# Channel attention: both convolutions back to back, attention product and final product behind them, Gram product last

## What is computed

```python
mu, var = mean and variance of x over (C, H, W)      # per image
xn = (x - mu) * rsqrt(var + EPS) * ln_g + ln_b
Q, K, V = _proj(xn, ...)     # 12x12 product per head, then a 3x3 depthwise convolution, each with bias
logits = einsum('bhnc,bhnd->bhcd', K, Q) / alpha     # 8 heads of 12 channels
attn = softmax(logits, axis=-1)
out = einsum('bhnc,bhcd->bhnd', V, attn)
return einsum('bcij,oc->boij', out, w_f) + b_f + xn
```

## Time and profile before

| | |
|---|---|
| median of 3 runs | 544.88 us (543.45 to 545.36) |
| the profiled execution | 541.99 us |
| its span | 540.5 us |
| PE busy in the span | 527.2 us (98%) |
| DVE busy | 366.9 us (68%) |
| ACT busy | 318.4 us (59%) |
| POOL busy | 165.4 us (31%) |

### The profile page before, as it was taken

One profiled execution on the slowest core, in us unless ns is written; L12 is line 12 of the kernel. 1 busy time (PEld: TensorE's weight loads), 2 busy tenths in 40 slices (PEclk: granted clock), 3 DMA queues, 4 the chain that ended last, 5 costly groups with the idle time before them and its releaser, 6 DMA issues. The chain is left out here.

```text
span 540.5 us, 22584 instructions
## 1 busy us (share of the span) xinstructions
PE 527.2 (98%) x8570; PEld 335.2 (62%) x8570; DVE 366.9 (68%) x903; ACT 318.4 (59%) x781; POOL 165.4 (31%) x200
## 2 busy tenths in 40 slices
PE   8999999999999999989999999999999999999996
PEld 7777777777777777765334444458555555565553
DVE  2799999999999999964753232345556565656544
ACT  2488877777777778865993443423444444444432
POOL 8543344444434443430000000013443332333210
PEclk9999999999999999999999999999999999999998
DMA  4211111111110101000000000003454434444421
GB/s 83 55 39 42 30 30 30 29 29 29 29 29 24 26 23 43 1 4 0 0 1 0 0 0 0 0 6 83 116 154 126 113 101 116 123 111 108 114 51 32
DMA packets 36097, 26.09 MB, mean 48 GB/s; under 512 B 17241, under 2 KB 34777, under 8 KB 36057
## 3 DMA queue, kind: packets, MB, share of 16 engines
q1 hardware_dynamic: 32472, 19.81, 13.9%
q0 software_dynamic: 3584, 5.72, 4.6%
HBM read 18.36 MB, written 7.13 MB: 47 GB/s over the span
## 5 line engine op out<-in xcount | busy, mean ns | idle before, releaser
L359 POOL TENSOR_TENSOR scores<-scores,peak 128x768 f32<-128x768 f32 x64 | 94.2, 1472 | 128.5 <-DVE peak L502 128.5
L995 POOL DMA_DIRECT2D x_stack<-padded_x x96 | 52.2, 546 | 96.6 <-PE ps_v L1268 67.4
L419 ACT COPY probs_t<-ps_probs 128x768 f32<-128x768 f32 x64 | 51.1, 798 | 40.6 <-PE ps_probs L634 40.5
L494 DVE TENSOR_TENSOR scores<-ps_scores,bias 128x768 f32<-128x768 f32 x64 | 61.3, 957 | 6.1 <-PE ps_scores L624 4.3
L502 DVE TENSOR_REDUCE peak<-scores 128x12 f32<-128x768 f32 x64 | 61.0, 953 | 2.4
L647 PE MATMUL ps_out<-v_blocks,probs_t 128*64 128x54 f32 x1536 | 57.2, 224 | 1.6 <-ACT out_t L424 1.5
L647 PEld LDWEIGHTS ps_out<-v_blocks,probs_t 128*64 128x64 f32 x1536 | 50.2, 138 | 12.9 <-issue 12.9
L846 ACT ACTIVATE hidden<-ps_hidden,fc_b_folded 128x512 f32<-128x512 f32 x48 | 32.4, 688 | 42.9 <-PE ps_hidden L798 42.7
L413 ACT ACTIVATE scores<-scores 128x768 f32<-128x768 f32 x64 | 54.2, 847 | 1.5 <-POOL scores L359 1.5
L634 PE MATMUL ps_probs<-ident,scores 128*128 128x128 f32 x384 | 54.3, 277 | 0.0
L881 DVE SCALAR_TENSOR_TENSOR mixed<-ps_y,fc_b,stream 96x384 f32 (+3 forms) x32 | 13.9, 476 | 54.1 <-PE ps_y L805 54.1
(11 more groups left out here) (137 smaller groups left out, 915.4 us busy)
## 6 DMA issues: line engine op xcount, KB each, us to landing
x_stack<-padded_x SPq DMA_DIRECT2D x96, 54.0 KB
x_stack<-padded_x POOLq DMA_DIRECT2D x96, 54.0 KB, 2.7
padded_x<-x_pad SPq DMA_DIRECT2D x32, 121.5 KB, 2.5
out<-y_sb SPq DMA_DIRECT2D x32, 96.0 KB, 2.0
x_now<-in_x SPq DMA_DIRECT2D x32, 72.0 KB, 1.8
stream<-in_x SPq DMA_DIRECT2D x32, 72.0 KB, 1.9
x_now<-in_x SPq DMA_DIRECT2D x32, 24.0 KB, 1.8
stream<-in_x SPq DMA_DIRECT2D x32, 24.0 KB, 1.8
```

The source lines that it names most:

```text
L359: nc.gpsimd.tensor_tensor(sc, sc, peak[:, par, p, :].unsqueeze(2).to_broadcast((128, HEADS, WN)), ALU.subtract).then_inc(s["shifted"], 1)
L419: nc.scalar.copy(probs_t[:, :], ps_turned).then_inc(s["turned_copied"], 1)
L494: nc.vector.tensor_tensor(scores[:, par, p, :].rearrange("p (g c) -> p g c", g=NG), ps_scores[:, :, 0:GROUP * WN], bias[:, p, :].rearrange ...
L995: engine.dma_start(x_stack[64 * half + i * HC:64 * half + (i + 1) * HC, slot, :, :], rows).then_inc(landed[slot], 16)
```

## The change

The PE step for t becomes: both convolutions of image t + 1, `attend(t - 1)`, `finalise(t - 2)`, `turn_tokens(t + 1)`, the waits for image t + 2, and `gram(t)`. The first tokens are turned ahead of the loop; the final product is one image later than before. The other engines follow: ACT does the exponential of image t - 1 first and the copy of `ps_av` last, DVE copies tokens last and ends image t - 2, SP stores image t - 2. `v_sb` has four buffers and not two. No arithmetic changes.

```diff
-    v_sb = sb("v_sb", [128, 2, ROUNDS, N])
+    v_sb = sb("v_sb", [128, SLOTS, ROUNDS, N])
...
             if not past(t + SLOTS):
                 gather(sp, t + SLOTS, lap + 1, slot, 0, stacked_sp)
-            if not is_image(t, 0):
-                store(t - 1, 1 - slot % 2)
+            if not is_image(t, 0) and not is_image(t, 1):
+                store(t - 2, slot % 2)
             if not past(t + AHEAD):
                 write(t + AHEAD, (slot + AHEAD) % SLOTS)
         lap_loop(sp, step)
+        store(B - 2, 0)
         store(B - 1, 1)
...
-        def copy_v(t, par):
+        def copy_v(t, slot):
             act.wait_ge(s["v_ready"], t + 1)
-            need(act, s["av_ready"], t - 1)
-            nc.scalar.copy(v_sb[:, par, :, :], ps_v).then_inc(s["v_copied"], 1)
+            need(act, s["av_ready"], t - SLOTS + 1)
+            nc.scalar.copy(v_sb[:, slot, :, :], ps_v).then_inc(s["v_copied"], 1)
...
         def step(t, lap, slot):                                   # ACT
             if not is_image(t, 0):
-                copy_av(t - 1)
-            if not past(t + 1):
-                copy_qk(t + 1)
-            exponent(t)
+                exponent(t - 1)
             if not past(t + AHEAD + 1):
                 take_moment(t + AHEAD + 1, (slot + AHEAD + 1) % 2)
             if not past(t + 1):
-                copy_v(t + 1, 1 - slot % 2)
+                copy_qk(t + 1)
             if not past(t + AHEAD):
                 pad_x(t + AHEAD, lap + (slot + AHEAD) // SLOTS, (slot + AHEAD) % SLOTS)
+            if not past(t + 1):
+                copy_v(t + 1, (slot + 1) % SLOTS)
+            if not is_image(t, 0):
+                copy_av(t - 1)
         lap_loop(act, step)
+        exponent(B - 1)
         copy_av(B - 1)
...
         def step(t, lap, slot):                                   # DVE
-            copy_tokens(t)
+            if not is_image(t, 0):
+                shift_logits(t - 1)
             if not past(t + AHEAD):
                 take_gain(t + AHEAD, (slot + AHEAD) % 2)
-            shift_logits(t)
+            if not is_image(t, 0):
+                normalise(t - 1)
             if not past(t + AHEAD):
                 take_offset(t + AHEAD, (slot + AHEAD) % 2)
-            normalise(t)
-            if not is_image(t, 0):
-                finish(t - 1, lap * 2 + (slot // 2 if slot % 2 else slot // 2 - 1), 1 - slot % 2)
-
+            if not is_image(t, 0) and not is_image(t, 1):
+                finish(t - 2, lap * 2 + slot // 2 - 1, slot % 2)
+            if not past(t + 1):
+                copy_tokens(t + 1)
+
+        copy_tokens(0)
         lap_loop(dve, step)
+        shift_logits(B - 1)
+        normalise(B - 1)
+        finish(B - 2, B // 2 - 1, 0)
         finish(B - 1, B // 2 - 1, 1)
...
+        turn_tokens(0)
+        await_taps(1, 0, 1)
+        pe.wait_ge(s["v_copied"], 1)
+
         def step(t, lap, slot):                                   # PE
-            turn_tokens(t)
-            if not past(t + 1):
-                await_taps(t + 1, lap + (slot + 1) // SLOTS, (slot + 1) % SLOTS)
-            if not is_image(t, 0):
-                attend(t - 1, 1 - slot % 2)
             if not past(t + 1):
                 convolve(t + 1, (slot + 1) % SLOTS, 0, ps_qk, s["qk_ready"])
-                pe.wait_ge(s["v_copied"], t + 1)
-            gram(t)
-            if not past(t + 1):
                 convolve(t + 1, (slot + 1) % SLOTS, 1, ps_v, s["v_ready"])
             if not is_image(t, 0):
-                finalise(t - 1)
+                attend(t - 1, (slot + 3) % SLOTS)
+            if not is_image(t, 0) and not is_image(t, 1):
+                finalise(t - 2)
+            if not past(t + 1):
+                turn_tokens(t + 1)
+            if not past(t + 2):
+                await_taps(t + 2, lap + (slot + 2) // SLOTS, (slot + 2) % SLOTS)
+                pe.wait_ge(s["v_copied"], t + 2)
+            gram(t)
 
         lap_loop(pe, step)
-        attend(B - 1, 1)
+        attend(B - 1, (B - 1) % SLOTS)
+        finalise(B - 2)
         finalise(B - 1)
```

More of the change, by code:

```diff
@@ L1296, in gram, with attend @@
             mm.then_inc(s["gram_ready"], 1)
-        def attend(t, par):
+        def attend(t, slot):
             pe.wait_ge(s["attn_ready"], (t + 1) * ROUNDS)
@@ L1302, in attend @@
             for r in range(ROUNDS):
-                mm = nc.tensor.matmul(ps_av[64 * r:64 * r + 64, :], attn[:, r, :], v_sb[:, par, r, :], start=True, stop=True)
+                mm = nc.tensor.matmul(ps_av[64 * r:64 * r + 64, :], attn[:, r, :], v_sb[:, slot, r, :], start=True, stop=True)
             mm.then_inc(s["av_ready"], 1)
```

## The result

The changed kernel takes 547.78 us (median of 6 runs, 546.83 to 552.49) against 543.89 us (6 runs, 542.41 to 545.36): a ratio of 1.0077 [1.0048, 1.0106]. It is slower by 3.9 us. The forecast was 544.0 us with a range up to 547.2, and "slower" had 0.23.

What follows compares the result with a forecast made beforehand. PE was taken as the bound, busy all 40.00 of 40 us at full clock. Span 522.5 + 15.5 = 538.0, plus 1.2 loop and 0.4 clock, 539.6 against 540.5; hence median 544.0, range 542.0 to 547.2.

Steps and rivals of the forecast that it cites:

- "slower": Whole kernel: the rivals that end slower, softmax ring as bound (0.15) and loop and tail at upper bounds (0.08).
- The steady step: PE's six groups per step in the new order: 4.74 us against 4.91, 0.17 less.
- The loop's own overhead: Branch between gram and qk at a lap's end: 0.25 us per lap, 0.2 for entering, 1.2 in all.
- The rival that the loop hides: Lap ends: branch costs nothing and the tail keeps 2.4 GHz, span 538.0, median 542.4; chance 0.27.
- "Does PE start to wait?": Steady step: PE stays covered by tenths, margin 0.4 us for attn ahead of av, 0.7 for v's copy.
- The ring rival: Softmax chain from av to next av, 4.42 us against 4.74, becomes the bound; 0.1 beyond gives 547.0; chance 0.15.
- "Gram, behind whose wait for this copy only gram stands": PE's wait for v's copy ahead of gram: gram due at 4.37 us, copy done about 3.7, margin 0.7.
- The end: From qk 31 on: two softmax chains in series, 15.5 us against 12.2, plus 0.4 for the clock.
- the clock's term: Tail: av 31 and y 30 at the lower clock cost 0.2 to 0.3 us each; 0.4 taken, bounds 0 and 1.0.
- The start, SP, POOL and the v buffers: Stage start: first step loses 0.4 us, qk 1 nothing; SP's store, POOL's gather and v's four buffers cost nothing.

Runs made afterwards that it cites:

- tokens2: The changed kernel with two token buffers, so the token copy need not wait for gram; 546.20 us, ratio 1.0027.
- the second execution: The changed kernel itself, unaltered, profiled and timed once more; 547.85 us, ratio 1.0041 to the kernel before.
- tail: The changed kernel with another order in the last step alone, gram 31 ahead of av 30; 544.86 us, ratio 1.0002.
- before_v4: The kernel before with four buffers for v and nothing else of the change; 544.94 us, ratio 0.9995.
- unroll: The changed kernel with the five laps of the loop written out; 557.02 us, ratio 1.0206.
- tokens2_tail_unroll: The changed kernel with two token buffers, the other order in the last step and laps written out; 551.46 us, ratio 1.0125.
- between_unroll: The changed kernel, laps written out, gram between the two convolutions, v-copy wait ahead of the tokens; 562.54 us, ratio 1.0348.
- before_unroll: The kernel before with its five laps written out; 545.73 us, ratio 1.0009.
- mid_unroll: The changed kernel, laps written out, gram between attention product and final product, v-copy wait ahead of the tokens; 546.04 us, ratio 1.0018.
- behind_unroll: The changed kernel, laps written out, gram directly behind both convolutions, v-copy wait ahead of the tokens; 545.50 us, ratio 1.0009.
- split_unroll: The changed kernel, laps written out, with the v-copy wait moved from ahead of gram to between the convolutions; 544.72 us, ratio 1.0011.
- its sibling: The changed kernel, laps written out, two token buffers, other last-step order, v-copy wait between the convolutions; 540.48 us, ratio 0.9912.

## Why the prediction was wrong, by its steps

**The steady step: right.** 4.74 was forecast and 4.744 measured, and each of its terms held to 0.02, the new borders among them: av to y 0.59 (0.58 forecast), tok to gram 0.53 (0.54). What lowers the step is that qk is followed by a group of its own shape. The Trainium skill, "TensorEngine Tiling (Array Packing)", Key Properties, says that this needs no drain while a change of mode does; the trace agrees, with 1.32 against 1.46. Over 28 steps this is 4.5 us, and it was there; it was spent elsewhere.

**The loop's own overhead: right in kind, a little high.** 0.25 a lap and 0.2 for entering were forecast, 1.2 in all. Measured are 0.26 at the first lap end, 0.19 at each of the other three and 0.08 at the entry, 0.9 in all. The rows of line 898 at a lap's end (ns, start) next to the timeline:

```profile
L898 PEldq ALU_OP  x1: 32/32/32, 484.9 to 484.9; - x1
L898 PEldq COMPARE_BRANCH  x1: 215/215/215, 485.0 to 485.0; - x1
L898 PEldq MOVE  x1: 29/29/29, 485.3 to 485.3; - x1
```

```profile
484.84 0.44 PE L1304 MATMUL ps_gram<-tokens 128*32 128x12 f32 x32
...
485.40 1.53 PE L1278 MATMUL ps_qk<-x_stack,conv_w 40*32 40x256 f32 x48
```

The sequence begins at 484.9, just behind gram's start, as worked out, and qk follows gram by 0.56 instead of 0.37. The rival that the loop hides is out.

**"Does PE start to wait?": this step failed, in a wait that it left out.** It placed the token copy 0.57 behind y_sb and gave av a margin of 0.4. But `copy_tokens(t + 1)` also needs gram t done, since there is one `tokens` buffer, and gram is now the last group of the step. So the copy starts 0.59 behind gram's start and ends 0.9 into the next step and not 0.77; peak and attn follow, and of the margin little is left. The ring rival had this chain in it, but through y_sb and not through gram. Waits by their sum, 400 to 520 us:

```profile
PEld ps_av L1313 <- DVE attn L1193: 7.0, 17, 0.4
DVE tokens L1174 <- PE ps_gram L1304: 6.5, 20, 0.4
```

Seventeen times the loads of av were held for attn, by up to 0.4; that is hidden behind v's matmuls, for v to av stays at 1.43 to 1.47. What shows is 0.07 once a lap, some 0.3 in all, and it comes to PE by the v copy and gram, as told under tokens2, which removes it. In price it was small in the loop; at the end it is 0.4 (below).

**"Gram, behind whose wait for this copy only gram stands": this sentence failed, and cost 2.0 to 2.8 us.** It gave the wait for the v copy a margin of 0.7. In a later lap it was 0.5 (489.26 against gram's start at 489.78), which costs nothing, and 0.4 once a lap, which costs the 0.07 above. But PE's sequencer stands at this wait until then, and behind it are gram and both convolutions. When it is released, 64 instructions are due within 0.37 us of gram, and then 192 more; the sequencer has no lead left, and where a packet of instructions ends inside v, v runs dry. Shown by the runs: in the loop it sits in the first lap (and in the second execution in two steps ahead of it) and in no later lap, it stands at the borders of packets, it grows to 13 us when all laps are new code, and it goes to nothing when the wait alone is moved one group later. Not explained is why the eight steps behind the loop, new code too, have none. That a lead is what is lost is the reading which fits all eight written-out kernels; the lead itself is in no row. This is the largest part by which the loop missed, 144.7 against 142.2: 2.0 for this, 0.3 for the tokens, 0.3 for the first two steps (4.14 and 4.50, forecast 4.06 and 4.24), 0.1 for 28 times 0.004, less 0.3 for the cheaper loop.

**The end: mis-sized, 17.9 for 15.9.** Its mechanism, two softmax chains in series, was right, and so were the two waits for attn. Against the working (15.5 and 0.4 for the clock) the terms came out so: the copy of tokens 31 stands behind gram 30 and starts 4.96 behind qk 31, forecast 4.46, which puts av 30 at 7.17 and not 6.75, 0.4 lost. The clock fell earlier than taken, at about 541, ahead of gram 31: y 29 and gram 31 take 0.81 and 0.62, and with what follows gram 31 this adds 0.4 up to av 31; av 31 to y 30 takes 1.05 and not 0.6. y 30 takes 1.17, and y 31 comes 1.83 behind it, where 1.15 was forecast. That one is not clock alone: y 31 waits for `y_sb` of image 30 (0.66 idle), because there is one `ps_y`, and the working had only the copy of av 31 in front of it. At the full clock y to the end of `y_sb` is 1.40, so about 0.3 of the 0.7 are a wait left out. From y 31 to the end it is 4.2 and not 3.8; 0.24 of this is y itself. Together 2.4 beyond the 15.5, of which 0.4 were allowed for: by this estimate 0.4 for the token copy, 0.3 for `y_sb`, about 1.4 for the clock and 0.2 behind the last y. The size of the clock's term was read from y 31 of the kernel before, 0.90 for 0.67; but there the clock fell while y 31 ran, and an av or y all at the lower level takes 0.5 more and not 0.2 to 0.3. tail shows the same groups at the high level with the gaps closed: 13.8.

**The start, SP, POOL and the v buffers: right.** Nothing measurable came of them; before_v4 is the test for the buffers.

Taken together: the forecast was 0.9 us of gain in the span (540.5 to 539.6); instead 3.6 are lost. The difference of 4.5 is 2.5 in the loop (2.0 of it the first lap) and 2.0 at the end (about half of it clock beyond the 0.4 allowed). The range ended at 547.2 since "slower" was thought of as a ring that runs in every step; the loss came mostly from two places that are passed once.

## What to carry to other kernels

A wait whose data is in time can still cost: ask what stands behind it on that engine's sequencer, put it directly ahead of the instruction that needs it, and rather not in front of a long row of short instructions; compare the first lap with the later ones, and write the loop out, to see it. If gaps with no releaser move by a fixed number of instructions from step to step, compare their distance with the size of an instruction packet. For every group moved to the end of a step, list whose buffer it still holds and walk each copy that waits for it. Cost the tail as a schedule of its own, with the lower clock on everything behind the first long gap; the last step may have an order of its own, and here that was worth as much as the whole change cost.

## What the runs showed that was not expected

- PE can run out of instructions in new code, and does so where one 16,384-byte packet of 256 instructions ends and the next begins. Gaps of 0.2 to 1.0 us between matmuls (up to 1.4 between loads), put down to issue, appear inside v when a wait is released 0.35 to 0.86 us ahead of gram: lateness from the third step on is 13.0 us in unroll, 12.6 in tokens2_tail_unroll and 8.2 in between_unroll, 1.9 in before_unroll (1.24 us ahead), and 0.0 to 0.3 in mid_unroll, behind_unroll, split_unroll and its sibling, all with 0.74 or 0.75 MB of instructions. In unroll and tokens2_tail_unroll the clock at 0.50 for 3.4 and 6.8 us in the middle of the stage is part of this, at most 1.7 and 3.4 us.
- The granted clock drops to 0.50 behind a wait of 2.35 us in a stretch where PE was busy 2.65 of 5 us, and stays there to the end. With waits of at most 0.69 between PE's groups its mean over the end was 0.98 (tail).
- Moving the branch from behind gram to behind v hid it in the later laps (nothing that shows and not 0.19) without making the kernel faster.
